# The three mask loads of an iteration: issued by SyncE ahead of the index spread instead of by ScalarE

## What is computed

```
x = norm(chunk_attention(q=ctx, k=ctx, v=ctx) * mask + x)     # 16 chunks of 64, 8 heads of 16; keys with mask <= 0 get -1e9
x = x + lora_attention(x, ctx)                                # 32 heads of 32, 8 groups of keys and values
x = norm(chunk_attention(q=ctx, k=ctx, v=ctx) * mask + x)     # other weights
out = neighbour_aggregate(ctx, x, k=30)                       # 30 nearest columns of ctx, 3 coordinates turned
                                                              # spherical, an MLP with batch norms over all samples,
                                                              # a softmax over the 30, a weighted sum of rows of x
```

## Time and profile before

| | |
|---|---|
| median of 3 runs | 8279.92 us (8253.25 to 8283.1) |
| profiled execution | 8271.05 us |
| its span, first to last instruction | 8269.3 us |
| mean granted TensorE clock in the span | 0.859 of 2.4 GHz |
| busy: PE, DVE, ACT, POOL | 6884.4, 6179.9, 4307.4, 2685.8 us |

### The profile page before, as it was taken

How to read it: one execution, slowest core, us unless ns; L and a number is a source line. 1 busy time by engine, 2 the same in 40 slices (tenths; PEclk the granted TensorE clock), 3 DMA queues, 4 the chain that set the end, 5 groups by cost and what they waited for, 6 DMA issues and landing times.

```text
span 8269.3 us, 204463 instructions
## 1 busy us (share of the span) xinstructions
PE 6884.4 (83%) x79422; PEld 4925.1 (60%) x79422; DVE 6179.9 (75%) x8508; ACT 4307.4 (52%) x9907; POOL 2685.8 (32%) x3399
## 2 busy tenths in 40 slices
PE   8888888888888888888888888888888759588888
PEld 5555555555555556555555555655555523488888
DVE  5777777777777777777777777777777747777777
ACT  3555555555555555555555555555555404566666
POOL 2333333333333333333333343333333310111111
PEclk9888888888888888888888888888888779899999
DMA  2111111111111111111111111111111130222222
GB/s 99 55 57 57 55 55 55 55 55 55 55 55 58 58 56 55 55 55 55 55 55 55 55 60 59 56 57 55 59 60 56 63 85 11 68 66 67 65 59 61
DMA packets 295563, 482.41 MB, mean 58 GB/s; under 512 B 103250, under 2 KB 216034, under 8 KB 293698
## 3 DMA queue, kind: packets, MB, share of 16 engines
q1 hardware_dynamic: 240205, 372.00, 15.1%
q10 hardware_dynamic: 54133, 94.55, 3.6%
HBM read 393.25 MB, written 73.25 MB: 56 GB/s over the span
## 4 chain that ended last, share of the span: by engine, by line
PE 54%; DVE 16%; ACT 15%; issue 10%; POOL 2%; DMA 1%; ACTq 1%; DVEq 0%; SPq 0%; POOLq 0%
ACT S L1047 6%; PE SCA L842 6%; PE PD L959 5%; PE SCA L811 4%; PE MISC L664 4%; PE SCA L946 3%; DVE m L1353 3%; ACT kexp L1090 3%; PE TP L834 3%; DVE pd L1359 3%; PE SCB L946 2%; PE PD L639 2%; PE SCA L682 2%; PE SCA L786 2%; PE TP L778 2%
## 5 line engine op out<-in xcount | busy, mean ns | idle before, releaser
L1353 DVE MAX8 m<-pd 128x8 f32<-128x1024 f32 x1024 | 1249.3, 1220 | 210.8 <-ACT pd L1016 99.0
L509 POOL TENSOR_TENSOR prod<-prod,hm 128x480 f32<-128x480 f32 x384 | 406.1, 1057 | 2928.8 <-ACT prod L1041 2762.2
L1357 DVE FIND_INDEX8 idx<-m,pd 128x8 uint32<-128x1024 f32 x1024 | 1248.7, 1219 | 9.5 <-issue 9.5
L1359 DVE MATCH_REPLACE8 pd<-m,pd 128x1024 f32<-128x1024 f32 x768 | 929.8, 1211 | 0.0
L639 PE MATMUL PD<-arena 128*128 128x512 f32 x1028 | 660.8, 730 | 149.7 <-ACT pd L1016 127.5
L664 PEld LDWEIGHTS MISC<-ptab,gat 128*128 128x128 bf16 x23400 | 673.8, 99 | 107.1 <-issue 77.7
L1600 DVE TENSOR_TENSOR gat<-maskT,con 120x2048 f32<-120x2048 f32 x256 | 592.1, 2352 | 171.2 <-PE SCA L946 162.3
L664 PE MATMUL MISC<-ptab,gat 128*128 128x24 bf16 x23400 | 667.5, 176 | 35.4 <-DVE gat L1309 20.6
L1047 ACT ACTIVATE S<-SCA,mx 128x64 f32<-128x64 f32 (+1 forms) x2560 | 572.0, 380 | 233.1 <-DVE mx L1365 233.1
L1365 DVE TENSOR_REDUCE mx<-SCA 128x16 f32<-128x1024 f32 (+1 forms) x192 | 235.2, 1225 | 506.9 <-PE SCA L767 456.1
L1047 ACT ACTIVATE S<-SCB,mx 128x64 f32<-128x64 f32 (+1 forms) x2560 | 570.9, 381 | 0.0
(11 more groups left out here) (270 smaller groups left out, 15192.6 us busy)
## 6 DMA issues: line engine op xcount, KB each, us to landing
gat<-low_scratch SPq DMA_DIRECT2D x396, 640.0 KB, 4.2
arena<-in_ctx ACTq DMA_DIRECT2D x33, 512.0 KB, 3.9
maskT<-in_mask ACTq DMA_DIRECT2D x32, 512.0 KB
arena<-in_x ACTq DMA_DIRECT2D x32, 512.0 KB, 6.3
x_scratch<-arena ACTq DMA_DIRECT2D x32, 512.0 KB, 4.8
x3T_scratch<-arena ACTq DMA_DIRECT2D x32, 512.0 KB, 3.7
arena<-x3T_scratch SPq DMA_DIRECT2D x32, 512.0 KB, 7.0
arena<-x_scratch SPq DMA_DIRECT2D x32, 512.0 KB, 9.3
```

The lines of the kernel that those rows point to most:

```text
L1353: step(V.max(m, buf[:, :]))
L1357: last = V.max_index(idx[:, t, 8 * r:8 * r + 8], m, buf[:, :])
L1359: step(V.match_replace(buf[:, :], m, buf[:, :], -3.0e38))
```

## The change

SyncE issues the three loads at the top of its own loop, ahead of `spread`, behind a wait on a new semaphore `mask_free`. VectorE increments it once before the loop, and once in each iteration when the masked output of layer 2 (L1400) is written. ScalarE's three issues are gone. Sizes, tiles and `mask_ld` are as before.

```diff
@@ -192,6 +192,7 @@
 
         hm_ready, norm_done, ot_ready = (sem(n) for n in ("hm_ready", "norm_done", "ot_ready"))
         pick_step = sem("pick_step")
+        mask_free = sem("mask_free")
         dve_step, v2_evac, front_done, topk_done, oproj_used, xl_done, var_done = (sem(n) for n in (
             "dve_step", "v2_evac", "front_done", "topk_done", "oproj_used", "xl_done", "var_done"))
         xx_step, xx_parts = sem("xx_step"), sem("xx_parts")
@@ -323,6 +324,13 @@
                                  .partition_broadcast(P)).then_inc(oh_ld[n % NOH], 16)
 
             with sp.Fori(0, NB) as i:
+                mrow = mask_in[i, :, :]
+                halves = mrow.rearrange("a (c h k) -> a c h k", h=2, k=CHUNK)
+                sp.wait_ge(mask_free, i + 1)
+                for h in range(2):
+                    sp.dma_start(mb[96 + 3 * h:99 + 3 * h, :].rearrange("p (c k) -> p c k", k=CHUNK),
+                                 halves[0, :, h, :].partition_broadcast(3)).then_inc(mask_ld, 16)
+                sp.dma_start(maskT[:, :], mrow[0, :].partition_broadcast(P)).then_inc(mask_ld, 16)
                 spread(i, (i + NB - 1) % NB, (i + NB - 3) % NB)
             spread(NB, NB - 1, NB - 3)
             store_spherical(NB, NB - 2)
@@ -1124,12 +1132,6 @@
 
 
 
-                    mrow = mask_in[i, :, :]
-                    halves = mrow.rearrange("a (c h k) -> a c h k", h=2, k=CHUNK)
-                    for h in range(2):
-                        act.dma_start(mb[96 + 3 * h:99 + 3 * h, :].rearrange("p (c k) -> p c k", k=CHUNK),
-                                      halves[0, :, h, :].partition_broadcast(3)).then_inc(mask_ld, 16)
-                    act.dma_start(maskT[:, :], mrow[0, :].partition_broadcast(P)).then_inc(mask_ld, 16)
                     chunk_attention(0)
 
 
@@ -1284,6 +1286,7 @@
         def _(dve):
             V = nc.vector
             dve.sem_inc(nb_used, 1)
+            dve.sem_inc(mask_free, 1)
             V.memset(V1[:, :, HD:HD + 1], 1.0)
 
             for n, (W, kc, w) in enumerate(WCHUNKS):
@@ -1400,6 +1403,8 @@
                     V.scalar_tensor_tensor(y[:, :], SC[0][:, :], bof[:, b:b + 1], maskT[:, :], ALU.add, ALU.mult)\
                         .then_inc(oproj_used, 1)
                     dve.wait_ge(oproj_used, i * 3 + l + 1)
+                    if l:
+                        dve.sem_inc(mask_free, 1)
                     if l == 0:
                         dve.wait_ge(x_ld, i * 16 + 16)
                     step(V.tensor_tensor(y[:, :], y[:, :], x_res[:, :], ALU.add))
```

## The result

The changed kernel took 8276.85 us (median of 20 runs, 19 of them between 8233.39 and 8299.39), the kernel before, beside it, 8242.8 us (20 runs, 8150.45 to 8298.78). The ratio is 1.0056 (95% interval 1.0034 to 1.0077): **slower by 0.56%**, where 0.27% faster was forecast. The three shown ahead of the prediction are among the 20 of before; their median stood 37 us too high in a spread of 148 us. The ratio is one of means and leaves out one disturbed run of the changed kernel (18532.88 us, clock 0.312) and the four runs of before that lie over 1.5% above its fastest; with all 20 of before it is 1.0041, slower all the same.

A forecast was written before the change was run, and what follows sets the result against it. No engine alone bounds the kernel; hand-overs within an iteration do, with GpSimd's path limiting the gain. 25.9 us gained less 3.5 for VectorE's increment gave 22.4 us (0.27%) less, 8257 us, range 8215 to 8288.

The forecast's parts named there:

- The main term: ScalarE's loop head loses three load issues, 1.31 us an iteration; where GpSimd does not decide, 25.9 us gained in all.
- three kinds of iterations: By ScalarE's third-group wait for TensorE: none, GpSimd decides (6 iterations); about 0.4 us (4); 1.4 us or more (21).
- the clock following up: TensorE's shorter idle gap at each head raises the granted clock, 40 us more gain, 8217 us; chance 0.20.
- rival 4: SyncE's loads come late, so VectorE waits for the mask at L1420; 1 in 100, within 0.07 shared with Rival 3.
- its own sign of being wrong: Among the signs listed against the forecast: mean granted clock over the loop moved by more than 0.01.
- Rival 3: Longer TensorE wait at the neighbour products costs clock in 10 iterations, 60 us, 8319 us; 0.07 with rival 4.
- That wait: TensorE's neighbour products waiting for ScalarE's eviction in iteration 10: 1.14 us before, forecast to become 2.45 us.
- rival 1: Less TensorE idle time at iteration heads tips a third of iterations to the faster clock: 8217 us; chance 0.20.
- GpSimd as a fixed floor: GpSimd's path to its first neighbour sum was taken as independent of the mask loads, limiting ScalarE's gain.
- VectorE's increment: Added semaphore increment between L1400 and L1405: 0.10 to 0.11 us, 32 times, 3.5 us lost.
- The steps costed at nothing: SyncE's added wait and three issues, and the mask transfers about 13 us earlier on its queue: cost 0.
- The base: Median of the three runs shown of the kernel before, 8279.92 us, from which the forecast was subtracted.

The follow-up runs named there:

- e18: Changed kernel with another semaphore's (nb_used) first increment moved from VectorE to SyncE, second run: 8244.21 us, 1.0020 of the kernel before.
- e17: Kernel of e18 plus ten small spare copies at ScalarE's loop head, putting the keys 1.05 us later: 8210.22 us, 0.9996 of the kernel before.
- e2: Changed kernel, unmodified, repeated on chip 1: 8290.41 us, 1.0073 of the kernel before.
- e13: Changed kernel, unmodified, repeated on chip 2: 8273.87 us, 1.0058 of the kernel before.
- e9: Changed kernel, unmodified, repeated on chip 3: 8243.49 us, 0.9972 of the kernel before.
- e7: Changed kernel with mask_free's first increment on SyncE and one unused increment (pad) ahead of GpSimd's loop: 8182.35 us, 0.9878 of the kernel before.
- e16: Kernel of e7 run again, on the same chip: 8201.61 us, 0.9980 of the kernel before.
- e3: Changed kernel with mask_free's first increment made by SyncE instead of VectorE, chip 1: 8238.76 us, 1.0006 of the kernel before.
- e11: Kernel of e3 run again, on chip 3: 8226.78 us, 0.9945 of the kernel before.
- e12: Changed kernel with another semaphore's (nb_used) first increment moved from VectorE to SyncE, chip 3: 8234.13 us, 0.9954 of the kernel before.
- e14: Changed kernel plus five small spare copies at ScalarE's loop head, putting the keys 0.6 us later: 8284.23 us, 1.0084 of the kernel before.

## Why the prediction was wrong

- **The main term was right in size.** The steps on ScalarE and its three kinds of iterations summed to 25.9 us. e18 against e17 isolates ScalarE's time and gives 25.7 to 33 us at an equal clock, by the slope used, for 1.05 of the 1.3 us. Against the whole change, -22.4 was forecast, and -19.5 measured at an equal clock over all occasions, -10 to -26 on single ones. In the traces the third group's eviction comes 47.1 and 47.0 us after GpSimd's first cast in the two executions of before, and 46.6 to 46.8 in the four of the changed kernel. That 25.9 and 25.7 are so near is luck: the second holds a GpSimd step that the first had no term for.
- **The step that failed** is not one that I costed but one that I held still. The forecast stood on the clock staying as it was, with 0.20 for the clock following up and 0.07, shared with rival 4, for it going down; its own sign of being wrong, a clock that moves by more than 0.01, is what came. Against the kernel before beside it, it was lower by 0.0125 (e2) and 0.0140 (e13), which costs 61 and 68 us, three times the gain, and equal in e9. In the runs of the result the clock of before is not recorded; its median of 8242.8 stands where the line has 0.865, against 0.8556 of the changed kernel.
- **Rival 3 had the mechanism in kind**, and the price, 60 us, but too small a chance. I put the harm into a longer idle time of TensorE behind the neighbour products. That wait was to grow to 2.45 us, and was 0.47 in iteration 10. What the windows show is earlier: TensorE enters its first transposes 1.15 us sooner, and the slow stretch over them mostly ends 6 us later. But e17 and e18 differ in this too, and in both the time at 1.2 GHz from 25 to 50 us is the same; they part behind 150 us. So no run shows the step by which the clock is lost, only that ScalarE's microsecond sets it off (e17, e18), and that it need not (e7, e16). The earlier trace rows had the hint: two kinds of iterations 9 us apart, with clocks of 0.88 and 0.84. What tips an iteration from one kind to the other was worth more than all else in it.
- **The rule named with rival 1** (the Trainium skill, "TensorE: Matmul & The Clock Gate", Part 1) I read as saying that less idle time can only help. In e2 and e13 waits at the head were shorter and the clock was lower; the traces do not agree with that reading. Whether it fails because of when the activity comes, no run shows.
- **GpSimd as a fixed floor** was wrong by 0.55 us: its sum comes 45.22 us after its start, not 44.67. The step that grew by 0.77 us has VectorE's comparisons beside it, which came 1.1 us earlier in the mean with ScalarE's work; in e17, where they lie 0.9 us later than in e18, it is short again. I had seen no wait between the two and counted them as independent.
- **VectorE's increment**: 0.11 us, as forecast, but the step missed what the same edit did to the place of the code: 0.29 us more in the last index search. Together 0.4 us an iteration instead of 0.11, 13 us by their length. What removing the gap gives at an equal clock is not settled: 26 us in e3 against e2, and 4 to 5 us the other way in e11 and e12 against e9.
- **The steps costed at nothing** on SyncE and the transfers held.
- **The base** was three runs of a kernel whose runs spread over 148 us. The 30 us from 8253.25 to 8283.1 in those three should have widened the range. The measured 8276.85 lies inside my range of times, 8215 to 8288, only because that base was 37 us too high; it is luck, and the sign is wrong.

**Open:** what makes the kernel before fall into its short iterations on some occasions and not on others (0.8565 and 0.8694 on the same chip), what kept e14 out of them, by which step the clock falls, and whether e17 and e18 part where before has a low clock. That a kernel can have the clock without giving the time at the head back is shown by e7 and e16, which have GpSimd's pad and not the gap.

## What to carry to other kernels

In a loop whose iterations differ by several us through the granted clock alone, a shift of 1 us at the head can cost more through the clock than it gains. Add up the slow time stretch by stretch over whole iterations and many of them: one slow stretch that ends early may be followed by another, and a single pair of iterations misleads. Give "the clock moves against me" a chance that fits what the kinds of iterations differ by. Compare kernels over many runs on more than one occasion and put time against clock: the line separated some 20 us of gain from 60 of loss, where any single comparison showed only their sum. Its slope and the occasion are part of the uncertainty, not only the scatter. And an engine's first and last instructions in a loop are worth a look when a change adds even one instruction ahead of it.

## What was not expected of the hardware

- The sign of the same comparison, same programs, changed with the occasion: 1.0056 (1.0041 with all runs of before), 1.0073, 0.9972, 1.0058.
- GpSimd's 128x480 step took 1.92 us with 0.88 us of VectorE's bf16 comparisons (128x2560) beside it, and 2.77 with 1.35 us; but 1.83 with 1.04 us in e17.
- e7 and e16 ran at 0.8686 and 0.8666 with the slow stretch at the head ending late in most iterations; e14 ran at 0.8564 with it ending early in 18 of 30.
- One instruction ahead of GpSimd's loop removed 4.3 us an iteration from its path: the 2.55 and 2.2 us between its register instructions at the loop head became 0.27 and 0.09. One ahead of VectorE's loop moved a 0.3 us gap between two instructions. The Trainium skill ("Runtime: NRT & Kernel Launch", Instruction fetch mechanics) calls the cost of crossing into the next block of instructions mostly hidden, and warns of a stall where a taken branch leads out of what is held. The gaps at GpSimd's loop head stand behind its branch and agree with the second in kind; that they are fetches no run shows.
